# Query, key and value projections of an attention block, as three products of rounded parts

## What is computed

```python
h = layernorm(x)                                   # (2, 2048, 128)
q = einsum('bsd,dhk->bshk', h, Wq) + bq            # 16 heads of 64
k = einsum('bsd,dhk->bshk', h, Wk) + bk
v = einsum('bsd,dhk->bshk', h, Wv) + bv
attn = softmax(einsum('bqhd,bkhd->bhqk', q / sqrt(64), k))
out = einsum('bqhd,hdm->bqm', einsum('bhqk,bkhd->bqhd', attn, v), Wo) + bo
x = x + layernorm(out)
x = x + layernorm(gelu(layernorm(x) @ U1 @ V1 + b1) @ U2 @ V2 + b2)
```

## Time and profile before

| | |
|---|---|
| median of three runs | 2408.31 us |
| the profiled execution, its own time | 2408.61 us |
| its span, first to last instruction | 2406.8 us |
| TensorE matmul busy (records, ends modelled) | 2363.3 us, 98% |
| ScalarE busy | 2140.5 us, 89% |
| VectorE busy | 2044.8 us, 85% |
| GpSimd busy | 2033.3 us, 84% |
| mean granted TensorE clock | 0.994 of full |

### The profile page before, as it was taken

The page is one execution under the profiler, slowest core; times in us unless marked ns, Lnnn a source line. Parts: engine busy times, 40 slices in busy tenths (PEclk is TensorE's granted clock), DMA queues, the critical chain, the costliest instruction groups (busy, mean ns, idle before and its releaser), DMA issues.

```text
span 2406.8 us, 44126 instructions
## 1 busy us (share of the span) xinstructions
PE 2363.3 (98%) x15628; PEld 1158.0 (48%) x15628; DVE 2044.8 (85%) x3249; ACT 2140.5 (89%) x2427; POOL 2033.3 (84%) x1141
## 2 busy tenths in 40 slices
PE   6999999999999999999999999999999999999998
PEld 3444444445445454444445444454444545444444
DVE  7888888888888888888888888888888888888977
ACT  5999999898998999999998999999999998989976
POOL 4888888888888888888888888888888888889986
PEclk8999999999999999999999999999999999999999
DMA  1100001000000000100001000100000000110101
GB/s 51 28 15 28 28 15 33 28 14 28 28 20 28 28 14 28 34 15 27 28 15 33 28 15 27 33 21 22 28 27 21 28 27 15 35 29 21 36 27 36
DMA packets 62973, 62.59 MB, mean 26 GB/s; under 512 B 28868, under 2 KB 46660, under 8 KB 62756
## 3 DMA queue, kind: packets, MB, share of 16 engines
q1 hardware_dynamic: 61748, 59.44, 8.3%
q10 hardware_dynamic: 1008, 0.33, 0.1%
HBM read 56.88 MB, written 2.61 MB: 25 GB/s over the span
## 4 chain that ended last, share of the span: by engine, by line
PE 92%; DVE 3%; POOL 2%; ACT 2%; issue 1%; DMA 0%; POOLq 0%; ACTq 0%; DVEq 0%
PE o_ps L428 35%; PE spare_ps L390 13%; PE score_ps L407 11%; PE score_ps L410 9%; PE score_ps L413 9%; PE spare_ps L376 3%; PE spare_ps L367 3%; PE spare_ps L358 3%; PE spare_ps L473 3%; POOL total L1113 2%; PE spare_ps L440 1%; DVE max_part L838 1%; ACT probs L664 1%; ACT score_ps L654 0%; DVE ln_stats L804 0%
## 5 line engine op out<-in xcount | busy, mean ns | idle before, releaser
L1113 POOL TENSOR_TENSOR total<-total,probs 128x832 f32<-128x832 f32 (+1 forms) x896 | 1761.9, 1966 | 294.1 <-ACT probs L664 216.9
L838 DVE TENSOR_REDUCE max_part<-spare_ps 128x1 f32<-128x512 f32 x2027 | 1302.2, 684 | 310.5 <-PE spare_ps L390 294.4
L664 ACT ACTIVATE probs<-score_ps 128x1024 f32<-128x1024 f32 x1024 | 993.7, 1023 | 219.1 <-PE score_ps L413 217.0
L654 ACT ACTIVATE score_ps<-m_all 128x1024 f32<-128x1024 f32 x1024 | 1012.1, 1032 | 14.4 <-DMA m_all<-m_scratch 14.4
L428 PE MATMUL o_ps<-probs,v_sb 128*64 128x512 f32 x4096 | 974.9, 597 | 0.0
L428 PEld LDWEIGHTS o_ps<-probs,v_sb 128*64 128x64 f32 x4096 | 271.5, 137 | 423.5 <-issue 278.3
L390 PE MATMUL spare_ps<-k_hi,q_hi 64*128 64x512 f32 x2027 | 455.8, 445 | 11.7 <-DVE max_part L838 8.3
L407 PE MATMUL score_ps<-q_hi,k_hi 64*128 64x512 f32 x2048 | 426.9, 413 | 1.2 <-ACT score_ps L654 1.2
L413 PE MATMUL score_ps<-q_hi,k_lo 64*128 64x512 f32 x2048 | 405.3, 391 | 0.0
L410 PE MATMUL score_ps<-q_lo,k_hi 64*128 64x512 f32 x2048 | 404.7, 391 | 0.0
L390 PEld LDWEIGHTS spare_ps<-k_hi,q_hi 64*128 64x128 f32 x2027 | 194.1, 184 | 424.4 <-issue 239.8
(11 more groups left out here) (131 smaller groups left out, 926.4 us busy)
## 6 DMA issues: line engine op xcount, KB each, us to landing
m_all<-m_scratch SPq DMA_DIRECT2D x64, 512.0 KB, 4.3
denom<-denom_scratch SPq DMA_DIRECT2D x122, 128.0 KB, 2.9
m_scratch<-neg_rows SPq DMA_DIRECT2D x256, 1.0 KB
y_acc<-in_L_attn_x SPq DMA_DIRECT2D x8, 256.0 KB, 5.9
xg<-in_L_attn_x SPq DMA_DIRECT2D x8, 256.0 KB, 2.8
block_out<-probs SPq DMA_DIRECT2D x8, 256.0 KB, 2.3
denom_col<-denom SPq DMA_DIRECT2D x61, 4.0 KB
denom_scratch<-denom_col SPq DMA_DIRECT2D x61, 4.0 KB, 1.4
```

Source lines behind the costliest of these rows:

```text
L654: nc.scalar.activation(score_ps[st % 2][:], m_all[:, G % 2], ACT.Copy).then_inc(s["seed_done"], 1)
L664: nc.scalar.activation(probs[:, st % RING], score_ps[st % 2][:], ACT.Exp, scale=SCALE).then_inc(s["exp_done"], 1)
L838: nc.vector.reduce_max(max_part[:, G % 2, h, qt, kc:kc + 1], bank[max_bank(n, h)], AX.X).then_inc(s["max_done"], 1)
L1113: nc.gpsimd.tensor_tensor(others(total[:, G % 2], G), so_far, others(probs[:, st % RING], G), ALU.add).then_inc(s["sum_done"], 1)
```

## The change

Rows and weights are split into a rounded part (`x_hi`, `w_hi`, type float32r) and the rest (`x_lo`, `w_lo`, float32r). Each projection becomes three float32r products accumulated in one bank: `w_hi` with `x_hi`, `w_lo` with `x_hi`, `w_hi` with `x_lo`, each on all 128 columns of the array in place of two halves. ScalarE's copy now writes `x_hi`; VectorE makes `x_lo` (eight times); GpSimd makes `w_hi` and `w_lo` for each of the eight pairs. Keys wait for `w_split` in place of the weights' DMA. To make room, `xnT`, `xn` and `xnT2` go: the tail's `xn`, `xnT2`, `hT` and the output tiles move into `v_sb` and `probs`, the late normalised rows into `q_parts`, and the first `xn` and its transposes move from doubles 479 and 480 to 483 and 484.

```diff
-WEIGHTS_AT = 2
+WEIGHTS_AT, SPLIT_AT = 2, 3
...
-XN = [479, 487, 495, 501, 505, 507]
-XT = [480, 488, 496, 502, 507, 509]
+XN = [483, 487, 495, 501, 505, 507]
+XT = [484, 488, 496, 502, 507, 509]
...
-        xnT = sb("xnT", [P, B * S])
+
+        x_hi = sb("x_hi", [P, B * S], F32R)
+        x_lo = sb("x_lo", [P, B * S], F32R)
...
         w_qkv = sb("w_qkv", [P, 2, 3, P])
+        w_hi = sb("w_hi", [P, 2, 3, P], F32R)
+        w_lo = sb("w_lo", [P, 2, 3, P], F32R)
...
+        old_values = v_sb[:, 0].rearrange("p t n -> p (t n)")
+        xn = old_values[:, 0:2 * CH].rearrange("p (g t d) -> p g t d", g=2, t=TC)
+        xnT2 = old_values[:, 2 * CH:4 * CH].rearrange("p (g n) -> p g n", g=2)
...
-        hT = [v_sb[:, 0].rearrange("p t n -> p (t n)").rearrange("p (f n) -> p f n", f=FF // P),
-              xnT[:, 0:S].rearrange("p (f n) -> p f n", f=FF // P)]
+
+        hT = [probs[:, 4 * k:4 * k + 2].rearrange("p r h n -> p (r h) n") for k in range(2)]
...
         def normalised_x(g):
-            return first_xn[:, g] if g < NC else xn[:, g % 2]
...
+        FIRST_LO_AT = {0: 1, 3: 2, 6: 3}
...
-                    pe.wait_ge(s["xnT_done"], k + 1)
+                    pe.wait_ge(s["x_split"], k + 1)
...
+            def project_parts(self, ps, slot, which, cols):
+
+                for k, (w, rows) in enumerate(((w_hi, x_hi), (w_lo, x_hi), (w_hi, x_lo))):
+                    last = nc.tensor.matmul(ps, w[:, slot, which, :], rows[:, cols], start=k == 0, stop=k == 2)
+                return last
+
             def project_k(self, u, c, name=None):
                 pe, b, slot = self.pe, u % B, u // B % 2
                 ps = self.take(name or SPARE["K", u * NC + c], "K", u * NC + c)
                 if c == 0:
-                    pe.wait_ge(w_in[slot], W_DMA_N * (u // B // 2 + 1))
+                    pe.wait_ge(s["w_split"], u // B + 1)
                 if u < B:
-                    pe.wait_ge(s["xnT_done"], u * NC + c + 1)
+                    pe.wait_ge(s["x_split"], u * NC + c + 1)
                 cols = slice(b * S + c * CH, b * S + (c + 1) * CH)
-                for h in range(2):
-                    last = nc.tensor.matmul(ps[half(h), :], w_qkv[:, slot, 1, half(h)], xnT[:, cols], start=True, stop=True)
-                last.then_inc(s["k_ps"], 1)
+                self.project_parts(ps, slot, 1, cols).then_inc(s["k_ps"], 1)
 
             def project_q(self, G, name=None):
                 u, c = G // NC, G % NC
                 b, slot = u % B, u // B % 2
                 ps = self.take(name or SPARE["Q", G], "Q", G)
                 cols = slice(b * S + c * CH, b * S + (c + 1) * CH)
-                for h in range(2):
-                    last = nc.tensor.matmul(ps[half(h), :], w_qkv[:, slot, 0, half(h)], xnT[:, cols], start=True, stop=True)
-                last.then_inc(s["q_ps"], 1)
+                self.project_parts(ps, slot, 0, cols).then_inc(s["q_ps"], 1)
 
             def project_v(self, u, t0, nt, name=None):
                 b, slot, at = u % B, u // B % 2, u * T + t0
                 ps = self.take(name or SPARE["V", at], "V", at + nt)
                 for t in range(nt):
-                    for k in range(2):
-                        at0 = b * S + (t0 + t) * P + k * HD
-                        last = nc.tensor.matmul(ps[half(k), t * P:(t + 1) * P], xnT[:, at0:at0 + HD],
-                                                w_qkv[:, slot, 2, :], start=True, stop=True)
+                    at0 = b * S + (t0 + t) * P
+                    for n, (w, rows) in enumerate(((w_hi, x_hi), (w_lo, x_hi), (w_hi, x_lo))):
+                        last = nc.tensor.matmul(ps[:, t * P:(t + 1) * P], rows[:, at0:at0 + P], w[:, slot, 2, :],
+                                                start=n == 0, stop=n == 2)
...
-                act.wait_ge(s["pv_done"], (UNITS - 1) * NC * T)
-            else:
+            if g == 0:
+                act.wait_ge(s["pv_done"], STEPS - RING + 2)
+                act.wait_ge(s["sum_done"], (CHUNKS - 1) * ADDS + T - RING + 1)
+                act.wait_ge(s["part_done"], STEPS // GROUP - 1)
+            elif g >= 2:
...
+            if g == NC:
+                act.wait_ge(s["first_split"], len(FIRST_COPIES))
...
-            nc.scalar.activation(xnT[:, g * CH:(g + 1) * CH], ps, ACT.Copy).then_inc(s["xnT_done"], 1)
+            nc.scalar.activation(x_hi[:, g * CH:(g + 1) * CH], ps, ACT.Copy).then_inc(s["xnT_done"], 1)
...
+        def dve_x_lo(dve, g):
+            dve.wait_ge(s["xnT_done"], g + 1)
+            ps = bank[FIRST_XT_BANK[g] if g < NC else SPARE["xnT", g]]
+            cols = slice(g * CH, (g + 1) * CH)
+            nc.vector.tensor_tensor(x_lo[:, cols], ps, x_hi[:, cols].bitcast(F32), ALU.subtract).then_inc(s["x_split"], 1)
...
+            if g == 0:
+                dve.wait_ge(s["pv_done"], (UNITS - 1) * NC * T)
...
+            dve_x_lo(dve, 0)
...
+                if n in FIRST_LO_AT:
+                    dve_x_lo(dve, FIRST_LO_AT[n])
...
+                if n in LATE_X_AT:
+                    dve_x_lo(dve, LATE_X_AT[n])
...
+            def split_weights(i):
+                j = i % 2
+                pool.wait_ge(w_in[j], W_DMA_N * (i // 2 + 1))
+                nc.gpsimd.tensor_scalar(w_hi[:, j], w_qkv[:, j], 1.0, None, ALU.mult).then_inc(s["w_high"], 1)
+                pool.wait_ge(s["w_high"], i + 1)
+                nc.gpsimd.tensor_tensor(w_lo[:, j], w_qkv[:, j], w_hi[:, j].bitcast(F32), ALU.subtract).then_inc(s["w_split"], 1)
+
             for g in range(NC):
                 first_rstd(g)
+                if g == 1:
+                    split_weights(0)
...
+                if u % B == 0 and c == 3 and d == SPLIT_AT and u // B + 1 < PAIRS:
+                    split_weights(u // B + 1)
```

More of the change, by code:

```diff
@@ L226, in build @@
         b2r = sb("b2r", [P, D])
-        xn = sb("xn", [P, 2, TC, D])
-        xnT2 = sb("xnT2", [P, 2, CH])
         q_parts = sb("q_parts", [P, 2, CH])
@@ L245, in build @@
             eps_added minus_mean stats_done mv_done rstd_done xn_done
-            xnT_ps_ready xnT_done first_copied first_split w_in0 w_in1 k_ps q_ps v_ps k_hi_done q_hi_done k_split q_split v_done
+            xnT_ps_ready xnT_done x_split w_high w_split first_copied first_split w_in0 w_in1 k_ps q_ps v_ps k_hi_done q_hi_done k_split q_split v_done
             m_out m_dma0 m_dma1 seed_done score_ready exp_done pv_done sum_done part_done merge_done tile_added denom_ps_ready
@@ L273, in z_tile @@
         def z_tile(g):
-            return probs[:, g // 2, g % 2, :].rearrange("p (t d) -> p t d", t=TC)
+            return probs[:, 2 + g // 4 * 4 + g % 4 // 2, g % 2, :].rearrange("p (t d) -> p t d", t=TC)
         def share(G):
@@ L280, in normalised_x @@
         def normalised_x(g):
-            return first_xn[:, g] if g < NC else xn[:, g % 2]
+            return first_xn[:, g] if g < NC else q_parts[:, g % 2].rearrange("p (t d) -> p t d", t=TC)
         def first_f32(kind, c):
@@ L699, in act_hidden @@
         def act_hidden(act, g):
-            if g < 2:
-                act.wait_ge(s["pv_done"], (UNITS - 1) * NC * T)
-            else:
+            if g == 0:
[3 more added lines that the diff above has]
+            elif g >= 2:
                 act.wait_ge(f["f_q_ps"], g - 1)
```

## The result

The changed kernel takes **2463.46 us** (median of four runs, 2462.66 to 2467.91) against 2408.31 us: a ratio of 1.0232, 95% interval 1.0219 to 1.0244. It is 55 us slower. 2461 had been forecast. The profiled execution took 2463.31 us with a span of 2461.5.

What follows compares the result with a forecast made beforehand. TensorE, 92% of the chain of waits, was taken to bound the kernel. From 2408.6 us: values +49, keys and queries +4, start +3, waits on ScalarE -3, giving 2461.6, median 0.3 below: 2461 us, own range 2440 to 2485.

Steps and rivals of the forecast that it cites:

- What bounds: Whole kernel: TensorE sets the pace with 92% of the chain of waits, ScalarE close behind; time added to TensorE reaches the end.
- A load of 128 columns prices a short product: Value projection: each float32r product is bound by its 0.107 us load, not 0.058 of streaming; 0.32 us a tile against 0.21 to 0.23.
- The second change of form: Around each projection on TensorE: two changes (64*128 to 128*128, then to 128*64) in place of one, costing 0.16 us more.
- The longer first load: First load after a change of form: stands open and is longer (192 ns against 141), raising the 0.16 us to 0.21.
- Keys and queries +4: Main loop, some 125 chunks: +0.05 us each, +6, of which the next double's wait on ScalarE's seeds swallows part, leaving +4 us.
- Values +49: Value insertions: 84 of one tile at +0.26 us, 70 of two at +0.34, seven of four at +0.52; together +49 us.
- -3 elsewhere: Loop: 3 us taken off because some doubles behind an insertion of values already wait on ScalarE's seeds.
- The start +3, bounds 0 to 7: Ahead of the loop: first keys wait for x_lo (+0.7 us), three more x_lo add 2.2, shorter first projections return under 1.
- The splits of weights and moved buffers at zero: GpSimd's seven later splits: zero, +14 us with no cover; tail's moved buffers: zero, bounds -2 and +3.
- Short products dearer: Rival, value products: 128-column float32r streams in four passes, 0.215 us each; values cost 140 us, total 2553 us; chance 0.14.
- open loads: Rival, all projections: each load waits for the matmul before it, 0.107 or 0.058 us more per product; 2545 us; chance 0.04.
- no drain: Rival, before projections: change from 64*128 to 128*128 is free for float32r; about 2407 us, or 2377 with shorter loads; faster 0.07, even 0.03.

Runs made afterwards that it cites:

- e4: Changed kernel, but value products stream only the first 64 columns of weights, their loads of 128 columns kept; 2459.86 us.
- e7: Changed kernel, but each tile of values has two products, the one of w_hi with x_lo left out; 2436.93 us.
- e6: Changed kernel, but all three projections are one float32 product on all 128 columns, x_hi read as float32, x_lo left out; 2466.37 us.
- e8: Changed kernel, but all three projections back to float32 products in column halves on x_hi; x_lo and rounded weights made but unused; 2420.76 us.
- e1: Changed kernel, but values back to float32 products in column halves on x_hi; keys and queries stay three float32r products; 2417.56 us.

## Why the prediction was right

**What bounds: right.** TensorE's chain share rose from 92 to 94%, and what was added to it came out at the end.

**A load of 128 columns prices a short product: right.** e4 and e7 show that the moving columns don't set the price and that a product costs 0.105 to 0.111 us (forecast 0.107); that it is the load is read from the starts of loads. This is the term that decided the case. (The sum has +0.26 for one tile where 0.48 - 0.21 is 0.27: 1 us of 49.)

**The second change of form: right,** 0.16 us by e6 against e8. The longer first load that I had added to it, 0.05 us, shows in the keys: their first matmul stands 0.34 ahead of the second where the next distance is 0.24, 0.10 more; in the kernel before the same difference was 0.05 (0.48 and 0.43 us between the pairs of records). In sums it partly vanishes.

**Keys and queries +4: sign wrong, size small.** The double with keys is 0.04 longer, about as forecast, but the next one, which had waited for ScalarE's seeds, is 3.93 us where it was 3.98 to 4.00: all of the added time is swallowed and 1.7 us come out below zero. I had let the wait swallow a third.

**Values +49: 46.** Single doubles came out as forecast or slightly above; the doubles behind them swallow a part, which I had put into the sum as -3 elsewhere. The four terms of the loop give 50 by forecast and 45.8 by the marks.

**The start +3, bounds 0 to 7: too small, 9.3 in the changed kernel's profile and 8 to 13 over all profiles with its order.** This is the term that was mis-sized. I added up operations (three `x_lo`, 2.2 us, first keys 0.7) and not the ring that they close: a projection waiting in TensorE's queue holds back the maxima behind it, and VectorE idles 4.3 us. The granted clock, which differs too, was not in the sum either. Of the first split of weights I had said that it ends about with `x_lo`; it ended 0.4 us after it, since it can't begin before the last DMA at 10.49, which the kernel before needed only at the projection itself.

**The splits of weights and moved buffers at zero: right,** 0.4 us over 56 chunks in e8, and +1.3 and -1.9 in the last chunks and behind them.

So 2461 against 2463.5 holds partly because -4 in the loop and +6 at the start cancel.

**Rivals.** Short products dearer and open loads are excluded by the starts 0.11 apart and by e4 and e7, no drain by the keys' 3.09 and by e6. Halves in float32r, which would keep the form 128*64 and save the change, are in no run and stay open. No kernel of this study beats the one before; the nearest, e1, is 0.38% slower, and nearly all of that lies in the start.

## What to carry to other kernels

Count a matmul as the longer of its streaming and its load, as the records here bear out: with 128 moving columns, three float32r products with a load of 128 columns each (0.33 us a tile) lose to float32 in halves, whose records run side by side in pairs 0.11 us apart, two pairs a tile (0.21 to 0.23). Count changes of form too, 0.16 us each here, and read both from the starts of records around an existing insertion of the same form. When a new operation is put between two queues at a kernel's start, follow the ring it closes, not its duration; and before gathering small insertions, look at what the other engine does in the doubles left empty.

## What was not expected of the hardware

A float32r matmul of 512 columns holds the engine 0.23 to 0.24 us, and a quarter of the float32 projection of the same columns is 0.215, so three products save less than a quarter of it: 0.70 against 0.86 us. At the lower granted clock ahead of the loop the float32r matmul takes 0.43 us, no more than its 512 columns at 1.2 GHz (starts at 25.01 and 25.43 us, where the granted clock is 0.50). The first keys have the same distance (13.48 and 13.91 us), though the profile gives a granted clock of 1.00 there; why the two differ isn't shown.
